# Adding 416 blocks into an adjacency matrix: where each addition stands between the selects and the load of places

## The reference, cut to what matters

```
agg = segment_sum(x[src], dst)          # layer 0, and twice in layer 1
h   = (x @ W)[src] * edge_weight        # layer 2
agg = segment_sum(h, dst)
```

## Time and profile before

| | |
|---|---|
| median of three runs | 2282.49 us |
| the profiled execution | 2285.5 us |
| its span, first to last instruction | 2283.7 us |
| mean granted TensorE clock | 0.931 of full speed |
| busy: PE, DVE, ACT, POOL | 90%, 68%, 49%, 61% |
| the block stage, 389.4 to 694.8 us | 305.4 us |

### The profile page before, as it was taken

The page is one execution under the profiler, slowest core; times in us unless marked ns, Lnnn a source line. Parts: engine busy times, 40 slices in busy tenths (PEclk is TensorE's granted clock), DMA queues, the critical chain, the costliest instruction groups (busy, mean ns, idle before and its releaser), DMA issues.

```text
span 2283.7 us, 37069 instructions
## 1 busy us (share of the span) xinstructions
PE 2048.1 (90%) x7761; PEld 1159.7 (51%) x7761; DVE 1549.3 (68%) x4326; ACT 1122.1 (49%) x3234; POOL 1393.4 (61%) x1718
## 2 busy tenths in 40 slices
PE   4788794777889999999999799999999999999986
PEld 3444342555665555455444555555555555555545
DVE  8987666888885251111403588888888888888885
ACT  0476454777771010000010466666666666666654
POOL 1477886444446888888885466666666666666530
PEclk9698797777779999999999899999999999999999
DMA  5410321000002121121120233333333333333321
GB/s 193 158 16 3 88 69 17 0 0 0 0 0 65 39 44 20 21 62 20 29 54 12 78 98 98 98 100 100 99 100 98 98 98 98 99 99 101 93 67 46
DMA packets 75080, 147.01 MB, mean 64 GB/s; under 512 B 26829, under 2 KB 37570, under 8 KB 74631
## 3 DMA queue, kind: packets, MB, share of 16 engines
q0 software_dynamic: 44704, 95.66, 17.3%
q1 hardware_dynamic: 27356, 45.20, 6.0%
q10 hardware_dynamic: 2946, 5.28, 0.6%
HBM read 123.11 MB, written 22.40 MB: 64 GB/s over the span
## 4 chain that ended last, share of the span: by engine, by line
PE 68%; DVE 10%; POOL 10%; issue 7%; DMA 2%; DVEq 2%; ACT 2%; ACTq 0%; SPq 0%; POOLq 0%
PE ps L910 24%; PE ps L653 11%; POOL pair_table L529 10%; PE ps L672 9%; PE ps L848 4%; PE ps L893 3%; PE ps L895 3%; PE ps L894 3%; PE ps L896 3%; DVE adj_t L1432 2%; PE ps L801 2%; DVE adj_t L1232 1%; DVE dense L1418 1%; DVE dense L1419 1%; DMA pair_table<-dense 1%
## 5 line engine op out<-in xcount | busy, mean ns | idle before, releaser
L910 PE MATMUL ps<-adj_t 128*128 128x512 f32 x1288 | 615.2, 600 | 14.3 <-DVE adj_t L1641 14.3
L1124 ACT ACTIVATE adj_t<-adj_t 128x128 f32<-128x128 f32 x966 | 315.3, 389 | 211.6 <-DVE adj_t L1620 189.4
L594 POOL DMA_INDIRECT adj_t<-z_table,adj_t x322 | 313.3, 973 | 154.5 <-DVE adj_t L1630 68.5
L910 PEld LDWEIGHTS ps<-adj_t 128*128 128x128 f32 x1288 | 231.2, 189 | 249.8 <-issue 215.6
L529 POOL DMA_INDIRECT pair_table<-dense x192 | 236.2, 1230 | 131.2 <-issue 120.7
L543 POOL DMA_INDIRECT src_table<-st_two,src_rows x216 | 262.9, 1217 | 70.5 <-issue 65.2
L801 PE MATMUL ps<-dense 128*128 128x128 f32 x832 | 226.7, 385 | 0.0
L672 PE MATMUL ps<-wring,dense 128*128 128x512 f32 (+1 forms) x480 | 209.9, 599 | 4.6 <-issue 3.9
L1432 DVE TENSOR_TENSOR adj_t<-adj_t,ps 128x256 f32 x416 | 173.5, 417 | 53.4 <-PE ps L801 40.6
L893 PE MATMUL ps<-dense_r 128*128 128x512 f32 x322 | 200.3, 622 | 2.3 <-POOL dense_r L602 2.3
L602 POOL TENSOR_TENSOR dense_r<-adj_t,dense_r 128x512 fp32r<-128x512 f32 x81 | 104.6, 1291 | 156.1 <-ACT dense_r L1133 155.9
(11 more groups left out here) (276 smaller groups left out, 3835.1 us busy)
## 6 DMA issues: line engine op xcount, KB each, us to landing
src_table<-dense SPq DMA_DIRECT2D x8, 656.0 KB, 6.6
adj_t<-z_table,adj_t POOLq DMA_INDIRECT x322, 3.5
records<-dense SPq DMA_DIRECT2D x1, 5000.0 KB
adj_t<-src_table SPq DMA_DIRECT2D x73, 64.0 KB
adj_t<-zeros SPq DMA_DIRECT2D x1, 4576.0 KB
src_table<-st_two,src_rows POOLq DMA_INDIRECT x216
st_two<-records POOLq DMA_DIRECT2D x54, 62.5 KB
adj_t<-zeros SPq DMA_DIRECT2D x1, 3328.0 KB
```

Source lines behind the costliest of these rows:

```text
L594: g.indirect_dma_start(out=zg[:, s, c, :], out_offset=None, in_=z_table, in_offset=bass.IndirectOffsetOnAxis(ap=dsti[:, s, c:c + 1].bitcas ...
L910: last = mm(bank[6 + h], oh[:, c, :], msg[:, c, h * D:(h + 1) * D], start=c == c0, stop=c == c0 + count - 1)
L1124: last = A(msg[:, c, (2 + k) * P:(3 + k) * P], msg[:, c, MSG:MSG + P], ACT.Copy, scale=side[:, s, c, C_Y - ATT + k:C_Y - ATT + k + 1])
```

## The change

The select of a chunk now stands ahead of an addition, not behind it: select n + 7 ahead of addition n, where select n + 8 stood behind addition n. Apart from the turn's edge that is the same row of instructions. At the edge it is not: before, the load of places came right behind addition 15 and right ahead of addition 0; now a select can stand between addition 15 and the load. So that there is one, POOL's chunks are shifted: it makes chunks 1, 5, 9, ... in place of 3, 7, 11, ... Seven selects' worth (five of them DVE's) stand ahead of turn 0, and select 7 is the sixth.

```diff
-            for n in range(AB - 1, PAIR_CHUNKS, AB):
+            for n in range(1, PAIR_CHUNKS, AB):
...
-                    if c % AB == AB - 1:
+                    if c % AB == 1:
                         act.wait_ge(sel_pool, i * 2 + c // AB + 1)
                     else:
-                        act.wait_ge(sel_ready, i * (2 * AB - 2) + c - c // AB + 1)
+                        act.wait_ge(sel_ready, i * (2 * AB - 2) + c - (c + 2) // AB + 1)
...
             def turn(i, tail=False):
                 n0 = i * PLACES
-                _, block_at = nc.values_load_multi_w_load_instructions(
-                    pair_offs[0:1, ds(n0, PLACES)], engines=[mybir.EngineType.DVE], min_val=0, max_val=AW_COLS - P,
-                    skip_runtime_bounds_check_because="a sum of some of the steps between blocks; all of them make the last block's place")
                 for k in range(PLACES):
                     c, n = k % (2 * AB), n0 + k
+                    ahead = (c + 2 * AB - 1) % (2 * AB)
+                    if ahead % AB != 1 and (not tail or k + 2 * AB - 1 < PLACES):
+                        select(n + 2 * AB - 1, ahead)
+                    if k == 0:
+                        _, block_at = nc.values_load_multi_w_load_instructions(
+                            pair_offs[0:1, ds(n0, PLACES)], engines=[mybir.EngineType.DVE], min_val=0, max_val=AW_COLS - P,
+                            skip_runtime_bounds_check_because="a sum of some of the steps between blocks; all of them make the last block's place")
                     dve.wait_ge(blk_done, n + 1)
                     if not (isinstance(n, int) and n == 0):
                         dve.wait_ge(blk_added, n)
                     a = adj[:, :, ds(block_at[k], P)]
                     v.tensor_tensor(a, a, bank[c][:, 0:2 * P].rearrange("p (k n) -> p k n", k=2), ALU.add).then_inc(blk_added, 1)
-                    if c % AB < AB - 1 and (not tail or k < PLACES - 2 * AB):
-                        select(n + 2 * AB, c)
-
-            for c in range(2 * AB):
-                if c % AB < AB - 1:
+
+            for c in range(2 * AB - 1):
+                if c % AB != 1:
                     select(c, c)
```

## The result

| | before | after |
|---|---|---|
| median of six runs each, side by side | 2282.70 us (2280.07 to 2285.29) | 2291.88 us (2289.63 to 2293.62) |
| span of the profiled execution | 2283.7 us | 2290.7 us |
| mean granted TensorE clock | 0.931 | 0.927 |
| first to last addition | 302.84 us | 311.54 us |
| of it the 24 turns of the loop, their edges included | 281.47 us | 289.85 us |

The account below looks back on a forecast made before the run. DVE was taken to set the block stage's pace, with its sequencer late at the turn's edges. 24 edges at +0.30 us net gave +7.2, the last edge +0.1: 2282.5 + 7.3 = 2289.8 us, range for 8 in 10 2284.5 to 2295.

Parts of the forecast that it names:

- The edge in the loop: From addition 15 to the next turn's addition 0: handing over the select and its register instructions add 0.34 us an edge.
- The load starts when the sequencer reaches it: Load of places at the turn's edge: runs beside the engine and does not wait for DVE to finish its work.
- The waiting load: Rival, at the edge: the load waits until the select has run; +12.5 us, 2295.0 us; chance 0.08.
- the free select: Rival: the idle 0.2 us behind each taken branch lets the select go early, edge +0.1, about 2282.6 us; chance 0.12.
- The interval that loses its select: Within a turn, one interval falls from 0.66 to 0.62 us: 0.04 us gained a turn.
- The last edge: Written-out edge without register instructions: 0.15 us for the select's two halves, less 0.04, so +0.1.
- The start: Ahead of turn 0: six selects as before, addition 0 still starts when they are done; no change.
- POOL and ACT: Shifting POOL's chunks costs nothing, covered by POOL's 165.1 us wait for PE; ACT takes the same chunks in order.
- such waits: Sign of being wrong: additions waiting for matmuls of POOL's chunks.
- the work behind it: What follows the block stage, 1588.9 us: as long as before, with a width of 2 us allowed.

Follow-up runs that it names:

- e1_pool_shift: Kernel before, with POOL at chunks 1, 5, 9, ... and each select still behind its addition, select 7 ahead of the branch: 2289.26 us, ratio 1.0025.
- e2_load_first: Changed kernel with the load of places put ahead of the select at the edge, nothing else: 2289.64 us, ratio 1.0026 to the kernel before.
- e4_half: Changed kernel with the select at the loop's edges cut to its second half, so 24 of 416 blocks are wrong: 2288.70 us, one run.
- the padded pair: Changed kernel and kernel before, each with 28 one-element DVE writes ahead of its wait for the edges' data: 2286.23 us and 2278.30 us.
- e5_after_pad: Changed kernel with 28 one-element DVE writes ahead of the wait for the edges' data: 2286.23 us, ratio 1.0013 to the kernel before.
- e9_before_pad: Kernel before with 28 one-element DVE writes ahead of the wait for the edges' data: 2278.30 us, ratio 0.9979.
- e6_places32: Kernel before with 32 places a turn in place of 16: 2276.65 us, ratio 0.9971.
- e8_after32: Changed kernel with 32 places a turn in place of 16: 2282.45 us, ratio 0.9995 to the kernel before.
- the written-out kernel: Kernel before, or the changed arrangement, with DVE's block stage written out without a loop and places loaded four at a time: 2252.16 us and 2252.92 us.
- e11_loads_of_four: Kernel before with DVE's block stage written out without a loop and places loaded four at a time: 2252.16 us, ratio 0.9866.

## Why the prediction was right, and where it was off

Slower was forecast with a chance of 0.83, at 2289.8 us; it came to +9.2 and not +7.3 us, inside the range. By its own steps:

- **The edge in the loop**, taken as +0.34: +0.356 in the median, and the load's start +0.354. Right in size and in cause. e1_pool_shift and e2_load_first show that it is the sequencer's series and not the place of the load, e4_half that one half with its register instruction is 0.14 of it, and the padded pair that it is the same with the slow place gone (+0.355).
- **The load starts when the sequencer reaches it.** Right: in the changed kernel it starts 0.10 to 0.29 us before the select's second half has ended, at each of the 24 edges, and e2_load_first gave 0.469 against 0.821. The waiting load (+12.5) is thereby out, and the free select (an edge growing by less than 0.1) by the 0.356. The 0.2 us behind the taken branch, on which the free select was built, are 0.233 in both kernels; 0.1 of them belongs to the slow place, and no part of them hid the select.
- **The interval that loses its select**, 0.04 us gained a turn. Not gained. One of the intervals that became bare is the third, and it stayed at 0.725 where other bare ones take 0.617. The prediction had this as its unknown, "slow by 0.06 in the turn shown", with the possibility that it "grows to 0.1 without the engine's work to cover part of it", and yet took no change there, so that the 0.04 gained stood in the sum as if that interval were like the others. The term of 24 x 0.04 = 1.0 us was mis-sized: 0.2 was measured. e5_after_pad shows the larger part of the cause: with the code shifted the same interval takes 0.620. But in the padded pair too, 7.95 us more in the loop and 24 x 0.355 = 8.52 for its edges, only 0.6 is given back and not 1.0, partly since the interval behind a bare one takes 0.663 where others with a select take 0.656.
- **The last edge**, +0.15 for it: +0.08 (1.477 to 1.557). Slightly less; it weighs nothing.
- **The start**, taken as nothing: turn 0 is 0.48 us longer (9.79 to 10.27). Its first interval, where the addition waits for PE, is 391.66 - 390.67 = 0.99 us where it was 0.66, and ACT waits once for POOL, which it never did before:

```profile
390.67 0.42 DVE L1436 TENSOR_TENSOR adj_t<-adj_t,ps 128x256 f32 x1
...
391.66 0.42 DVE L1436 TENSOR_TENSOR adj_t<-adj_t,ps 128x256 f32 x1 [0.24 <-PE ps L801]
```

```profile
ACT dense L1058 <- POOL dense L556: 0.5, 1, 0.5
```

  Chunk 1 is now POOL's, its select is slower to come, and copy, matmul and addition of chunk 1 come late behind it. This is the one place where the wait for a chunk of POOL's made an interval longer; the prediction had named such waits as a sign of being wrong. The runs bear it out: with the shift ACT waits 0.47 us at this place and the first interval is 0.99 to 1.00 (e1_pool_shift, e5_after_pad), without it there is no wait and it is 0.66 (e9_before_pad, e6_places32). In e8_after32 ACT waits as well, but the longer first load holds addition 0 back by 0.4 us, and the interval is 0.66 again. The last turn gave 0.25 back (10.11 to 9.86).
- **POOL and ACT** in the rest of the stage, and **the work behind it**, nothing: 1588.51 us behind the last addition against 1589.30, within the 2 us that were left for it.

In sum: edges 24 x 0.356 = 8.5, the rest of the 24 turns 8.38 - 8.5 = -0.2 where -1.0 was expected, last edge +0.1, turn 0 and the last turn +0.2: the +8.70 of the stage. The medians of the runs differ by 0.5 more, which is within their interval. Of the 1.9 us by which the forecast was short, 24 x 0.016 = 0.4 are the edge's size, 0.8 the gain that didn't come, 0.2 the start and the end, and 0.5 lie between the profiles and the medians. Of the signs named ahead of time, the edges (2.21 and 1.56), the load's start and its 1.10 us came out; the loads are 12.10 us apart where 12.0 was forecast, and from the first load to the end of the last addition it is 314.1 us where 312.7 was.

The idea itself was to put the load of places where it is covered. But a load of 1.10 us is longer than the whole interval that it would have to hide in (0.62 us, of which DVE waits 0.21), and so every instruction put at the edge was added to it.

## What to carry to other kernels

Where an engine's sequencer is what is late, count its instructions in a row (handing over, register instructions, branches, register loads) and not the engine's work; moving one of them past another changed little here (0.06 us of 0.36), taking it to an interval in which the engine is what is waited for did. A register load that is too long to hide is cut into pieces that do hide: in the written-out kernel loads of 0.34 us disappeared, where one of 1.10 us with the branch beside it cost 1.2 us each time. The waits by releaser don't show this; the gap's start, the sequencer's rows in it and an equal interval without the load do.

## What the runs showed of the hardware

- The time of a register load by its size, with the row of one register from the last layer's loop in the kernel before; the others are 0.343 us for 4, 1.100 for 16, 2.103 for 32. One register takes 0.305, the next three add 0.013 each, and from there to 16 and on to 32 it is 0.063 each; where between 4 and 16 the price changes was not measured. All of them read SBUF. The Trainium skill, "Runtime: NRT & Kernel Launch", section "Instruction fetch mechanics", gives about 200 ns for a register, even in bulk. These loads are above that for one register, and well below it for each one beyond (1.100 us for 16 is 69 ns each).

```profile
L1634 DVEq TENSOR_LOAD <-src_offs x93: 299/305/323, 1317.9 to 2229.1; - x93
```

- Where a loop's code lies is worth 5 us here: 28 one-element writes ahead of the stage changed 2282.87 us to 2278.30, and 208 of them in another version lost 7.
- The granted TensorE clock of the stage rose as DVE's gaps went: 0.77 of full speed, 0.87 in e6_places32, and 0.92 in e11_loads_of_four, over nearly the same work, which here is its whole stage. Full speed is 2.4 GHz and the lower level 1.2, so these are mixtures of the two. PE was busy for 79% of the time in either (240.5 of 305.4 us; 216.4 of 273.5), with fewer long pauses: from the first to the last addition 25 of over 0.8 us in the kernel before, none in e11_loads_of_four. The gain is hardly due to the clock: the intervals between additions inside a turn are as long in the one kernel as in the other (0.656 and 0.663 with a select), and only the edges went. PE's busy time fell with the clock's rise.

```profile
388.00:661.50 273.50, 216.39 (x1248) 147.45 (x1248) 249.70 (x1039) 237.37 (x832) 131.25 (x208) 0.92 0.00 1
```
